# Keys stored with a third difference block on partitions 64 to 127, and an exponent pass that adds the maximum once in four steps

## The reference

```python
Q = xn @ W_q   # 16 heads of 16
K = xn @ W_k   # 4 heads of 16, as V = xn @ W_v
Qr, Kr = rope(Q), rope(tile(K, 4))
scores = einsum('bhqd,bhkd->bhqk', Qr, Kr) / 4
attention = (softmax(scores) @ tile(V, 4)) @ W_o
# experts: 8, the two with the largest router logits for each token, p their softmax
experts = sum over the two of p * ((clip(silu(xn @ Wg[e]), -7, 7) * (xn @ Wu[e])) @ Wd[e])
```

## Time and profile before

| | |
|---|---|
| median of 3 runs | 576.74 us (575.99 to 579.41) |
| the profiled execution | 576.07 us, of which the span from first to last instruction is 574.3 us |
| mean granted TensorE clock | 0.976 |
| TensorE matmul busy | 526.5 us, 92% |
| ScalarE busy | 383.5 us, 67% |
| VectorE busy | 396.3 us, 69% |
| expert tiles with rotation beside them | about 59 to 119 us |
| attention | about 232 to 572 us |

### The profile page before, as it was taken

The page is one execution under the profiler, slowest core; times in us unless marked ns, Lnnn a source line. Parts: engine busy times, 40 slices in busy tenths (PEclk is TensorE's granted clock), DMA queues, the critical chain, the costliest instruction groups (busy, mean ns, idle before and its releaser), DMA issues.

```text
span 574.3 us, 9921 instructions
## 1 busy us (share of the span) xinstructions
PE 526.5 (92%) x3464; PEld 249.3 (43%) x3464; DVE 396.3 (69%) x920; ACT 383.5 (67%) x548; POOL 173.2 (30%) x208
## 2 busy tenths in 40 slices
PE   1996748897999998999999999999999999999997
PEld 1832324454555554444444444444444444444433
DVE  4578756961666666587788887888888788785123
ACT  3421412431333433799999999999999999998673
POOL 3015854541222210012416422551344342600000
PEclk9997987897999999999999999999999999999999
DMA  8950235566642120310511421422224113100101
GB/s 293 375 184 1 80 133 170 169 183 193 170 138 74 59 62 29 103 38 19 131 47 45 115 58 41 102 65 75 57 58 119 31 57 84 30 2 21 46 29 55
DMA packets 39566, 53.72 MB, mean 94 GB/s; under 512 B 7936, under 2 KB 25728, under 8 KB 39520
## 3 DMA queue, kind: packets, MB, share of 16 engines
q1 hardware_dynamic: 32624, 40.25, 23.9%
q0 software_dynamic: 3408, 9.31, 5.9%
q10 hardware_dynamic: 3488, 3.55, 1.8%
HBM read 36.18 MB, written 16.65 MB: 92 GB/s over the span
## 4 chain that ended last, share of the span: by engine, by line
PE 73%; DVE 12%; DMA 6%; issue 3%; ACT 2%; SPq 2%; POOL 2%; DVEq 0%; ACTq 0%; POOLq 0%
PE bank L1249 21%; PE bank L1239 9%; PE bank L1112 9%; PE bank L1167 8%; PE bank L1129 7%; PE bank L1235 6%; PE bank L1184 4%; PE bank L1285 3%; DMA k_st<-rope_low 3%; PE bank L1122 2%; DMA rows_out<-xn 2%; DVE xn_t L907 2%; DVE xn L983 2%; SPq L378 1%; PE bank L1072 1%
## 5 line engine op out<-in xcount | busy, mean ns | idle before, releaser
L702 ACT ACTIVATE big<-bank 128x1024 f32<-128x1024 f32 x256 | 252.9, 1024 | 18.6 <-PE bank L1239 18.3
L1249 PE MATMUL bank<-big,v_st 128*32 128x256 f32 (+1 forms) x1472 | 148.3, 474 | 2.8 <-DVE xn L983 2.8
L1239 PE MATMUL bank<-qs,kb 64*128 64x512 f32 x512 | 120.0, 408 | 0.7 <-ACT big L702 0.7
L904 DVE TENSOR_REDUCE mx<-bank 128x1 f32<-128x512 f32 x128 | 87.8, 686 | 27.9 <-PE bank L1129 20.1
L899 DVE TENSOR_REDUCE mx<-bank 128x1 f32<-128x512 f32 x128 | 87.9, 687 | 22.1 <-PE bank L1114 20.0
L1167 PE MATMUL bank<-big,xn 128*128 x156 | 82.6, 654 | 15.9 <-ACT xn L671 15.4
L907 DVE CUSTOM_DVE_ANT_0 xn_t<-bank,xn_t 128x512 f32<-128x512 f32 x128 | 87.5, 684 | 4.5 <-PE bank L1129 1.5
L657 ACT ACTIVATE xn_t<-bank 128x512 f32<-128x512 f32 x128 | 76.7, 599 | 20.4 <-PE bank L1114 12.2
L1239 PEld LDWEIGHTS bank<-qs,kb 64*128 64x128 f32 x512 | 57.7, 185 | 19.4 <-ACT big L702 12.3
L1112 PE MATMUL bank<-ka,qs 64*128 64x512 f32 x128 | 63.4, 495 | 0.4 <-DVE mx L904 0.4
L1114 PE MATMUL bank<-ka,qs 64*128 64x512 f32 x128 | 63.3, 495 | 0.0
(11 more groups left out here) (140 smaller groups left out, 611.7 us busy)
## 6 DMA issues: line engine op xcount, KB each, us to landing
qs<-q_hl SPq DMA_DIRECT2D x64, 128.0 KB, 2.7
rows_out<-xn SPq DMA_DIRECT2D x39, 128.0 KB, 2.6
ka<-k_st SPq DMA_DIRECT2D x16, 256.0 KB
kb<-k_st SPq DMA_DIRECT2D x16, 256.0 KB
xs<-in_L_attn_x SPq DMA_DIRECT2D x4, 512.0 KB, 6.3
big<-in_L_ffn_Wg SPq DMA_DIRECT2D x16, 128.0 KB, 6.5
big<-in_L_ffn_Wu SPq DMA_DIRECT2D x16, 128.0 KB, 6.6
big<-in_L_ffn_Wd SPq DMA_DIRECT2D x16, 128.0 KB, 6.5
```

The lines of the kernel that those rows point to most:

```text
L702: act.activation(probs[kt % 2][:, 2 * j:2 * j + 2, :].rearrange("p r q -> p (r q)"), st_ps[j][:, :], ACT.Exp, scale=1.0 / math.sqrt(HD)).t ...
L904: nc.vector.reduce_max(mx[h][:, STEPS + k, 1:2], max_bank(v, i), axis=X_AXIS).then_inc(mx_taken, 1)
L1239: last = mm(out[i], kb[p][half[i], kt // QT, keys], qs[q][half[i], j, :], start=False, stop=True, skip_group_check=kt % 2 == 1)
L1249: last = mm(o_ps[32 * r:32 * (r + 1), columns], v_st[p][:, key_block(kt), :], probs[kt % 2][:, r, columns], start=(kt == 0 and columns.sta ...
```

## The change

A third difference, block 2-1, is made, and a fourth (3-2) beside it since the instruction covers two blocks. All four differences go to partitions 64 to 127 of the same 512 columns, so that a key part fills 128 x 512 as a query part does. `k_st` has 1024 columns in place of 768, and a key part is stored with eight DMAs of 64 x 512 in place of four of 64 x 768. `kb` now holds blocks 3, 0-2, 1-3 and 2-1, and the exponent pass goes through the blocks in the order 3, 1, 2, 0: it adds the maximum and block 3, then 1-3, then 2-1, then 0-2. The maximum is added once in four steps, so 128 of the 256 instructions of line 1235 go. `ka`, the maxima and the values are as before.

```diff
@@ -63,7 +63,7 @@
 
 
     q_hl = nc.dram_tensor("q_hl", [B, NH, 2 * HD, S], F32, kind="Internal").ap()
-    k_st = nc.dram_tensor("k_st", [B, KV, STACK, 2, KCOLS], F32, kind="Internal").ap()
+    k_st = nc.dram_tensor("k_st", [B, KV, STACK, 2, 2 * HALF], F32, kind="Internal").ap()
     xn_d = nc.dram_tensor("xn_d", [NT * P, D], F32, kind="Internal").ap()
     rows_out = nc.dram_tensor("rows_out", [SLOTS * P, D], F32, kind="Internal").ap()
 
@@ -93,10 +93,10 @@
         wo_s = sb("wo_s", [P, KV // 2, D])
         cos_s = sb("cos_s", [P, S])
         sin_s = sb("sin_s", [P, S])
-        rope_a = [sb(f"rope_a{m}", [P, KCOLS]) for m in range(3)]
+        rope_a = [sb(f"rope_a{m}", [P, HALF]) for m in range(3)]
         rope_b = [sb(f"rope_b{m}", [P, HALF]) for m in range(3)]
-        rope_hi = [sb(f"rope_hi{m}", [P, KCOLS], F32R) for m in range(3)]
-        rope_low = sb("rope_low", [P, 3, KCOLS], F32R)
+        rope_hi = [sb(f"rope_hi{m}", [P, HALF], F32R) for m in range(3)]
+        rope_low = sb("rope_low", [P, 3, HALF], F32R)
         rope_lo = [rope_low[:, m, :] for m in range(3)]
         stats = [sb(f"stats{h}", [P, TB, 6]) for h in range(2)]
         mean_var = [sb(f"mean_var{h}", [P, TB, 2]) for h in range(2)]
@@ -299,9 +299,6 @@
         def part_rows(q):
             return P if PARTS[q][1] < 2 else KV * HD
 
-        def part_cols(q):
-            return HALF if PARTS[q][1] < 2 else KCOLS
-
         def vector_cos(q):
 
             return PARTS[q][0] == BLOCKS - 1 or q in VECTOR_COS
@@ -313,7 +310,7 @@
 
         def stored_before(q):
 
-            return sum(32 if PARTS[o][1] < 2 else 64 for o in range(q % 3, q, 3))
+            return sum(32 if PARTS[o][1] < 2 else 128 for o in range(q % 3, q, 3))
 
 
         SHARED = 21
@@ -342,7 +339,7 @@
 
         def key_block(kt):
 
-            return kt // QT * QT + 2 * (1 - kt % 2) + kt // 2 % 2
+            return kt // QT * QT + (3, 1, 2, 0)[kt % QT]
 
         block = ctx.enter_context(nc.Block())
 
@@ -375,8 +372,9 @@
                     sp.dma_start(q_rows[1], rope_lo[n][:, 0:HALF].bitcast(F32)).then_inc(done, 16)
                 else:
                     for j, half in enumerate((rope_hi, rope_hi, rope_lo, rope_lo)):
-                        sp.dma_start(k_st[b, :, HD * j:HD * (j + 1), k % 2, :],
-                                     half[n][0:KV * HD, :].bitcast(F32)).then_inc(done, 16)
+                        for u in range(2):
+                            sp.dma_start(k_st[b, :, HD * j:HD * (j + 1), k % 2, u * HALF:(u + 1) * HALF],
+                                         half[n][KV * HD * u:KV * HD * (u + 1), :].bitcast(F32)).then_inc(done, 16)
 
 
             def store_y(t, i):
@@ -412,7 +410,7 @@
                 src = k_st[g // KV, g % KV]
                 for s in range(2):
                     sp.dma_start(kb[p][STACK * s:STACK * (s + 1), :, :].bitcast(F32),
-                                 src[:, :, QUART:KCOLS]).then_inc(kb_loaded[p], 16)
+                                 src[:, :, HALF - P:2 * HALF - P]).then_inc(kb_loaded[p], 16)
 
             def load_m(i):
 
@@ -644,12 +642,11 @@
             act.activation(in_tile[:, :, 1, :], hot_tile, ACT.Copy, scale=partition_no[:, 0:1]).then_inc(in_tile_ready, 1)
 
             def high_part(q):
-                n, rows_q = q % 3, part_rows(q)
+                n = q % 3
                 act.wait_ge(rope_done, q + 1)
                 if q >= 3:
                     act.wait_ge(qk_stored[n], stored_before(q))
-                act.activation(rope_hi[n][0:rows_q, 0:part_cols(q)], rope_a[n][0:rows_q, 0:part_cols(q)],
-                               ACT.Copy).then_inc(hi_ready, 1)
+                act.activation(rope_hi[n][:, :], rope_a[n][:, :], ACT.Copy).then_inc(hi_ready, 1)
 
             def take_gain(v, k):
 
@@ -844,19 +841,20 @@
                     else:
                         added.then_inc(k_summed, 1)
                         dve.wait_ge(k_summed, sum(PARTS[o][1] == 2 for o in range(q)))
-                        nc.vector.tensor_tensor(rope_a[n][0:rows_q, HALF:KCOLS], rope_a[n][0:rows_q, 0:QUART],
-                                                rope_a[n][0:rows_q, QUART:HALF], ALU.subtract).then_inc(rope_done, 1)
+                        nc.vector.tensor_tensor(rope_a[n][rows_q:P, 0:QUART], rope_a[n][0:rows_q, 0:QUART],
+                                                rope_a[n][0:rows_q, QUART:HALF], ALU.subtract)
+                        nc.vector.tensor_tensor(rope_a[n][rows_q:P, QUART:HALF], rope_a[n][0:rows_q, QUART:HALF],
+                                                rope_a[n][0:rows_q, P:P + QUART], ALU.subtract).then_inc(rope_done, 1)
 
             def rope_step(q):
                 if 2 <= q <= NP + 1:
-                    n, rows_q = (q - 2) % 3, part_rows(q - 2)
+                    n = (q - 2) % 3
                     dve.wait_ge(hi_ready, q - 1)
                     dve.wait_ge(rope_done, q - 1)
                     if q >= 5:
                         dve.wait_ge(qk_stored[n], stored_before(q - 2))
-                    cols_q = part_cols(q - 2)
-                    nc.vector.tensor_tensor(rope_lo[n][0:rows_q, 0:cols_q], rope_a[n][0:rows_q, 0:cols_q],
-                                            rope_hi[n][0:rows_q, 0:cols_q].bitcast(F32), ALU.subtract).then_inc(lo_ready, 1)
+                    nc.vector.tensor_tensor(rope_lo[n], rope_a[n][:, :],
+                                            rope_hi[n][:, :].bitcast(F32), ALU.subtract).then_inc(lo_ready, 1)
                 if q < NP:
                     (k, m), n, rows_q = PARTS[q], q % 3, part_rows(q)
                     if k < BLOCKS - 1:
@@ -1228,15 +1226,15 @@
                 out = [st_ps[j][:, i * HALF:(i + 1) * HALF] for i in range(2)]
                 half = [slice(STACK * i, STACK * (i + 1)) for i in range(2)]
 
-                first = 2 * (kt % 2) + kt // 2 % 2
+                first = (0, 2, 3, 1)[kt % QT]
                 keys = slice(first * P, (first + 1) * P)
-                if kt % 2 == 0:
+                if kt % QT == 0:
                     for i in parts:
                         mm(out[i], ones_r[half[i], :], ms[v][half[i], j, :], start=True, stop=False)
                 for i in parts:
                     if i == 1 and banks is not None:
                         pe.wait_ge(mx_taken, banks)
-                    last = mm(out[i], kb[p][half[i], kt // QT, keys], qs[q][half[i], j, :], start=False, stop=True, skip_group_check=kt % 2 == 1)
+                    last = mm(out[i], kb[p][half[i], kt // QT, keys], qs[q][half[i], j, :], start=False, stop=True, skip_group_check=kt % QT > 0)
                 if parts[-1] == 1:
                     last.then_inc(st_ready, 1)
 
@@ -1312,7 +1310,7 @@
                             pe.wait_ge(m_loaded[0], 64 * (g + 2))
 
 
-                        if kt % 2 == 0 and not last:
+                        if kt % QT < QT - 1 and not last:
                             scores(2 * p + h, h, p, kt + 1, s + 1, 0)
                             values_between(2 * p + h, h, p, kt, s, u, (u + 2, ahead, 1 - p, kt))
                             continue
```

## The result

| | before | after |
|---|---|---|
| median in the same session | 576.37 us (573.72 to 579.41) | 593.38 us (591.1 to 596.14) |
| the profiled execution, its span | 576.07 us, 574.3 us | 591.75 us, 590.0 us |
| mean granted TensorE clock | 0.976 | 0.971 |
| start of the attention, of the last two units, end | 231.7, 524.8, 574.3 us | 245.6, 542.2, 590.0 us |

The changed kernel takes 1.0309 times the time of the one before (95% interval 1.0272 to 1.0347), so it is 3.1% slower. The direction and the cause put first were forecast; the size was not. 1.8% was expected. The median of 593.38 us lies at the very end of the range of 582.5 to 594 us, and two of the four runs lie above it (595.01 and 596.14 us).

The account below looks back on a forecast made before the run. Bounds: key stores on four full DMA engines ahead of the attention, TensorE and ScalarE both nearly full in it. 576.07 + 9.6 + 3.2 - 0.3 - 1.8 = 586.8 us profiled, median 587; range 582.5 to 594.

Parts of the forecast that it names:

- the paragraph on the main attention: Main attention: 28 fours of maximum matmuls removed, 0.01 us each, 0.3 us gained (0 to 2.8), nothing added.
- The argument about `take_gain`: Main attention: the 0.47 us saved on TensorE becomes a wait for ScalarE's `take_gain`, so the values start no earlier.
- Parts 0 to 2: Key stores ahead of the attention: 3.2 us more for each part, so part 5 starts 9.6 us later (8.1 to 13.5).
- nearer to the bytes: Cost of a key part's stores: 3.2 us chosen between 2.7 by bytes and 4.5 by packets.
- the line through the packet times: Key stores' upper bound: 121 ns for a 3 KB packet, 96 ns for 2 KB, so 4.5 us more a part.
- Part 11: Later key store with a row store queued behind it: a further 3.2 us (2.7 to 4.5).
- The last two units: End of the attention: each of four removed fours saves 0.46 us, as no `take_gain` is there; 1.8 us gained.
- the extra issues: Four more DMA issues a key part, ahead of row stores and loads: nothing added, up to 2 us allowed.
- TensorE's order as the limit: Rival, main attention: a four saves 0.47 us, 32 fours 15.0 us; total 574.5 us, chance 0.08.
- Hidden stores: Rival, key stores: they spread or their waits have cover, at most 3 us come; 574.6 to 577.6 us, chance 0.13.
- A fixed price for each DMA or packet: Rival, key stores: packets or DMAs cost, not bytes; 7.7 us more a part, 31 in all, 605.7 us, chance 0.06.
- a fixed 2 us for each DMA in sequence: Key stores: 16 more DMAs would give 32 us; argued against because four stores land in 8.1 us, so overlap.

Follow-up runs that it names:

- the walk alone: Kernel before with only the maximum once in four steps, the new block order and interleaving in three of four steps; keys and stores unchanged: 589.38 us, ratio 1.0232.

## Why the prediction was right and wrong

**The step that failed** is the end of the paragraph on the main attention: "Nothing is added here, so no loss." The expected -0.3 us (0 to -2.8) became +3.5. Something is added: the condition for interleaving, 224 more value matmuls, and a second interleaved step in a row, which takes 2.63 us and not 2.46. With that condition put back the stage takes 292.0 us, inside the term's bounds; that it is 1.1 less than before says nothing, since one stall of VectorE and the scatter of the unchanged attention are as large. The argument about `take_gain` holds where it can be read, 1.61 against 1.62 us. I had followed the steps with kt = 1 and 5 and not asked which steps are made differently; the hunk stands at the end of the diff, and the prediction has no term for it.

**Parts 0 to 2** were named rightly and undersized: 11.1 us for 9.6, 3.7 for each part instead of 3.2, within the bounds of 8.1 to 13.5. The choice of "nearer to the bytes" was too near: in the one trace that parts them the bytes are 9.3 and the rest is 1.8, and the medians give the rest more. The row stores of before's second stretch, from which I drew the line through the packet times, are not key stores on four engines.

**Part 11** was +3.2 us and is +3.2 from issue to landing (19.3 for 16.1); 2.8 us of it arrive at the attention (13.9 less 11.1). That the two agree so closely is in part luck: with the same stores the way from the experts to the attention takes 183.4 and 184.9 us in two other kernels, for 186.1 here.

**The last two units** gained 1.7 us for a forecast of 1.8, as before with no `take_gain` to meet.

**The sum** in the profiled execution: 1.5 us more for parts 0 to 2, 0.4 less for part 11, 3.8 more for the main part, 0.1 less gained at the end. That is 5.0 us above 586.8, hence the 591.75. That a sum with one term missing still ended inside the range is due to its width. The range is also narrower than its terms: up to 2 us for the extra issues are allowed in the text and left out of its upper end, which would be 596 us with them. The median is another 1.6 us above the profiled execution. In the runs before, the median lay 0.3 above the profiled execution; this last microsecond is in no trace. Stalls as in the walk alone, in some executions, would do it, but that was not seen.

**The rivals.** TensorE's order as the limit (a four saves 0.47 us) is refuted by the 1.61 us. Hidden stores are refuted by the three waits of 9 to 11 us, and became true only when the layout spread them over sixteen engines. A fixed price for each DMA or packet, of 31 us in all, is refuted by the 13.9 us ahead of the attention, and by the eight stores with the old bytes, which add 1.8 us by their trace and 7.5 by their medians. The prediction's own argument against a fixed 2 us for each DMA in sequence does not hold: four stores would take 8 us by it as well, and 8.1 were measured. What refutes it is that eight stores with the old bytes take 8.26 and 8.19 us (78.10 to 86.36 to 94.55), where it would give 16.

**What a better version is.** The changed kernel with old interleaving and sixteen engines runs in 569.99 us, 1.4% faster than the kernel before. The kernel before with sixteen engines takes 571.12, so nearly all of it comes from the layout of the stores. The four-step walk by itself is worth the 0.35% of its own run, about the 1.7 us of the last two units.

## What to carry to other kernels

Give each hunk of a diff a term, those that change only a condition too, and count each line's instructions before and after; a changed order of TensorE costs time although the same products are made. When a transfer is in the chain while the average DMA share is low, divide the rate by the number of engines that it uses: the layout that spreads it is worth more here than the matmuls saved. Where the saved work only lets an engine reach its next wait sooner, look at who releases that wait before counting a gain. Before two profiled executions are compared stage by stage, compare a stage that neither kernel changes: here it differed by up to 4.5 us, enough to hide a loss of 1.6.

## What the hardware did that I had not expected

A wait for the end of a TensorE matmul can last about 1.1 us too long, and two engines that wait for different matmuls can be late together. With the new interleaving ScalarE was held so eight times with the keys of before and nine times on sixteen engines, VectorE with it in three and five of these, near the third step of a unit with gathers on GpSimd and DMA issues on SyncE going on at once. With the interleaving of before it was rarer, once in the kernel before and four times with its stores on sixteen engines, and VectorE alone was late. It went when either was moved a few microseconds, and the main part became 8.4 or 7.3 us shorter. What holds the engines back is not shown, and a mere shift in time as the cure is not excluded.

An issue of SyncE takes longer while stores on four engines are queued. The last issues of part 2, before and after:

```profile
76.97 2.77 SPq L378 DMA_DIRECT2D k_st<-rope_low  x2
...
87.38 5.63 SPq L376 DMA_DIRECT2D k_st<-rope_low  x4
```

That is 1.4 us for each DMA in both. All of parts 0 to 2 take 14.9 us for 12 DMAs before (64.86 to 79.74) and 28.2 us for 24 after (64.78 to 93.01), 1.2 us each. On sixteen engines the median is 0.60 us. So splitting did not make an issue slower, but there are twice as many of them, and the share of SyncE's queue in the chain goes from 2% to 4%. They did not set the pace: the last store of part 2 is issued before 93.01 and part 5 waits for it until 103.84. In the trace of the eight stores with the old bytes, which has as many issues, what they cost in parts 0 to 2 lies within 1.8 us.
